# Attention scores and their maximum pass in two float32r pieces, two heads in the halves of the array

## Chip, cores and metric

One core of a Trainium2 chip. The time is the device time of one execution in microseconds (us), the median of several.

## What is computed

`x` is (2, 2048, 256) in float32. Its layer norm goes through causal attention with 16 heads of 16 channels, and through a gated feed-forward block; both are added to `x`.

```python
qkv = einsum('btd,ed->bte', xn, w_in); q, k, v = heads(split(qkv))   # 16 heads of 16
att = einsum('bhqd,bhkd->bhqk', q, k) / 4
att = where(causal, att, 0.0)          # a masked score is 0, not minus infinity
out = softmax(att) @ v                 # so masked keys carry weight exp(0 - max)
r = sigmoid(xr @ W_r.T); k = relu(xk @ W_k.T) ** 2; ffn = r * (k @ W_v.T)
return x + out @ w_out.T + ffn
```

`xr` and `xk` mix each token with the one before it. Since masked scores are 0, the softmax runs over all 2048 keys, and its maximum is at least 0 in every row but the last.

## The kernel before

It has two stages, each a block of five instruction streams that meet by semaphores.

**The token stage** (`stage_tokens`) takes 4096 tokens in 8 chunks of 512. For each it forms the layer norm, turns it, makes q, k and v, and runs the feed-forward block; its matmuls are float32. Scores need more precision than one bf16 gives, so each q and k value is kept as three bf16 parts: ScalarE casts the high part (L602), VectorE subtracts (L513), ScalarE casts the middle part (L607), VectorE subtracts again (L518). The parts go to DRAM (`parts_d`).

**The attention stage** (`stage_attention`) works through 8 groups of 4 heads (`group`; 2 batches by 4 groups; `G` counts them, `p` is the buffer half, the other half is loaded for the next group). A group has 4 query chunks `u` of 512. Chunk `u` needs `4 * (u + 1)` key tiles `kt` of 128, so there are 40 steps in a group. The tiles on the diagonal are narrower: 512, 384, 256 and 128 queries.

In a step TensorE computes for each of 4 heads a score tile (L1090): 128 keys by up to 512 queries, a contraction over 99 rows: 6 products of parts (`Q_PARTS`, `K_PARTS`) of 16 channels, and 3 rows which add the negated row maximum, in three bf16 parts, against rows of ones. The tiles go to three PSUM banks in turn (`SRING`). ScalarE takes the exponential of each into `probs` (L972), a ring of 16. On diagonal tiles POOL clears a triangle (L920). Two steps later (`LAG`) TensorE multiplies the values in (L1104), four heads side by side in column strips of 32, in float32; a further column of ones gives the denominator. Behind the third score of a step stands this value product.

**The maximum pass.** A row's maximum must be known before its scores are computed. So every score is computed a second time with queries in rows: a *piece* (L236) is 128 queries by up to 512 keys of one head, contraction over 96 rows, into one of three banks `ps_m` (`MRING`; two banks in the token stage). VectorE reduces each piece to a column of maxima: a plain reduction (L251), or on the diagonal a fused mask, add and maximum (L247) followed by a read of the accumulator. A group has 160 pieces: 96 off the diagonal, all 512 wide, and 64 on it, 16 each of 128, 256, 384 and 512. `pieces_of` puts the pieces of a slot evenly among its score tiles: one slot is each chunk, and the last chunk of a group carries the first 80 pieces of the next group. The first 80 of the first group are made in the last four chunks of the token stage (`pieces_beside_tokens`). A piece matmul waits for the reduction three pieces back (`piece_reduced`), and the next score is queued behind it in TensorE's order.

When the pieces of a chunk are reduced, six small VectorE steps (`max_step`, L260 to L280) form the maximum and its three parts; TensorE turns them (L1067, bf16), ScalarE copies them out (L953), SP writes them as rows into `q_op` (`place_shift`, L819). Before the first group this is done for chunks 0 and 1 with nothing beside it.

**Other work of a chunk.** The masked keys of a diagonal tile need weight exp(-max): POOL spreads that over 16 diagonal matrices (L887), TensorE multiplies them in (`masked_keys`, L1114, 32 instructions), behind the value product that ends the chunk. It needs sums of values over later keys (`sum_suffix`, L1081 and L1082, into bank `ps_x`). VectorE then divides by the denominator (L1007 to L1018), SP stores the rows (`attn_t`). In the last group the output tiles (L1136) follow.

**SP's queue in a group**: shift rows of chunk 2, then the loads of the next group's q, k and v once the first chunk's output is done, the normalised rows, shift rows of chunk 3, shift rows of chunks 0 and 1 of the next group.

## Time and profile before

| | us |
|---|---|
| median of 3 runs | 1230.48 (1223.11 to 1233.08) |
| profiled execution | 1224.13 |
| its span | 1222.3 |
| TensorE, VectorE, ScalarE, POOL busy | 1127.3, 949.4, 743.4, 347.7 |
| mean granted TensorE clock | 0.98 of 2.4 GHz |

Busy times are unions of the instructions' durations on an engine. A matmul's duration has its fill and drain in it, so that back-to-back matmuls overlap; what one costs is the distance from start to start. A wait is put down to what came last.

### The profile page before, as it was taken

The page shows a single profiled execution, that of the slowest core. Times are in us where ns is not written, and L with a number is a line of the kernel's source. Part 1 is how long each engine was busy: PE and PEld are TensorE (multiplying, and loading weights), DVE is VectorE, ACT ScalarE, POOL GpSimd, SP SyncE. Part 2 cuts the span into 40 slices and gives each one's busy share as a digit, 9 for nine tenths or more (in the row PEclk, how much of TensorE's full clock was granted, in tenths as well). Part 3 has the DMA queues.
Part 4 walks back from the last instruction along what each step waited for, and adds up shares of the span by engine and source line. Part 5 has one row for each costly group of instructions (what it writes and reads, how often), then busy time and mean ns, then how long its engine had stood idle before and what let it go on. Part 6 is the DMA issues. An engine that isn't in the chain of part 4 may idle for free.

```text
span 1222.3 us, 21443 instructions
## 1 busy us (share of the span) xinstructions
PE 1127.3 (92%) x7168; PEld 459.4 (38%) x7168; DVE 949.4 (78%) x2433; ACT 743.4 (61%) x1553; POOL 347.7 (28%) x716
## 2 busy tenths in 40 slices
PE   5889888789999999999999999999999999999998
PEld 3656544343333333333333333333233332333345
DVE  5757888778689858986888788778968986899623
ACT  3544433166766666667667766766677666666773
POOL 2212113132423232334132323332332233224121
PEclk9999999889999989999999999999999999999999
DMA  4577732309001900180028002700360045002033
GB/s 129 164 185 172 213 109 91 104 3 144 9 2 23 130 6 2 24 129 6 2 32 122 6 1 39 114 6 2 53 100 6 1 60 94 6 1 79 6 108 108
DMA packets 62353, 79.22 MB, mean 65 GB/s; under 512 B 7075, under 2 KB 52515, under 8 KB 61219
## 3 DMA queue, kind: packets, MB, share of 16 engines
q1 hardware_dynamic: 61091, 73.66, 30.1%
q0 software_dynamic: 1152, 4.19, 1.2%
q8 instruction: 57, 0.93, 0.3%
q14 instruction: 53, 0.43, 0.1%
HBM read 43.78 MB, written 29.36 MB: 60 GB/s over the span
## 4 chain that ended last, share of the span: by engine, by line
PE 49%; DVE 12%; DMA 9%; issue 4%; SPq 2%; POOL 2%; ACT 1%; DVEq 0%; POOLq 0%
PE ps_o L1104 15%; PE ps_s L1090 14%; PE ps_m L236 13%; DMA v_sb<-vpad_d 9%; DVE part_max L251 5%; DVE ps_m L247 3%; PE ps_m L1136 2%; PE ps_o L1114 2%; POOL after L228 2%; DVE row_max L264 1%; PE ps_x L1081 1%; DVE part_max L247 1%; PE ps_x L1082 1%; DVE turned L1007 1%; SPq L200 1%
## 5 line engine op out<-in xcount | busy, mean ns | idle before, releaser
L972 ACT ACTIVATE probs<-ps_s 128x512 f32<-128x512 f32 (+3 forms) x1280 | 610.2, 534 | 290.0 <-PE ps_s L1090 285.1
L251 DVE TENSOR_REDUCE part_max<-ps_m 128x1 f32<-128x512 f32 x730 | 473.8, 680 | 33.7 <-PE ps_m L236 32.2
L1090 PE MATMUL ps_s<-q_op,k_op 99*128 99x512 bf16 (+3 forms) x1280 | 431.1, 355 | 8.8 <-ACT probs L972 6.0
L236 PE MATMUL ps_m<-k_op,q_op 96*128 96x512 bf16 (+3 forms) x1200 | 402.5, 355 | 33.5 <-DVE part_max L251 23.4
L247 DVE CUSTOM_DVE_ANT_0 ps_m<-ps_m,mask 128x384 f32<-128x384 f32 x470 | 229.2, 496 | 122.1 <-PE ps_m L236 120.4
L1104 PE MATMUL ps_o<-probs,v_sb 128*32 128x512 f32 (+3 forms) x2560 | 303.0, 546 | 4.8 <-POOL probs L920 4.8
L920 POOL TENSOR_SCALAR_AFFINE_SELECT probs<-probs 128x128 f32<-128x128 f32 x512 | 143.2, 296 | 396.3 <-ACT probs L972 389.6
L1090 PEld LDWEIGHTS ps_s<-q_op,k_op 99*128 99x128 bf16 x1280 | 122.0, 98 | 325.2 <-ACT probs L972 219.3
L236 PEld LDWEIGHTS ps_m<-k_op,q_op 96*128 96x128 bf16 x1200 | 117.9, 98 | 199.4 <-DVE part_max L251 92.6
L887 POOL TENSOR_TENSOR diag_weight<-ident,masked_weight 128x2048 f32<-128x2048 f32 x32 | 115.5, 3610 | 121.2 <-ACT masked_weight L939 121.2
L1104 PEld LDWEIGHTS ps_o<-probs,v_sb 128*32 128x32 f32 x2560 | 50.8, 108 | 94.0 <-issue 36.7
L228 POOL TENSOR_TENSOR after<-after,v_sb 128x64 f32<-128x64 f32 x120 | 40.0, 333 | 134.2 <-DMA v_sb<-vpad_d 125.4
L247 DVE DVE_READ_ACCUMULATOR2_ANT part_max<- 128x1 f32 x512 | 71.6, 140 | 0.0
L670 PE MATMUL ps_qk<-xn_t,w_in_sb 128*128 128x512 f32 x128 | 60.6, 609 | 1.7 <-ACT xn_t L597 1.4
L441 POOL TENSOR_TENSOR k_act<-k_act 128x1024 f32<-128x1024 f32 x8 | 15.4, 1919 | 126.5 <-ACT k_act L635 126.5
L602 ACT ACTIVATE parts<-ps_qk 128x512 bf16<-128x512 f32 x32 | 19.0, 594 | 46.7 <-PE ps_qk L670 46.7
L236 PE MATMUL ps_pieces<-k_op,q_op 96*128 96x512 bf16 (+2 forms) x80 | 25.6, 355 | 18.4 <-DVE part_max L251 9.2
L446 POOL TENSOR_TENSOR ffn<-ffn,x_in 128x512 f32<-128x512 f32 x16 | 21.5, 1342 | 57.8 <-DVE ffn L525 57.8
L607 ACT CAST parts<-rest 128x512 bf16<-128x512 f32 x32 | 19.7, 616 | 28.9 <-DVE rest L513 28.9
L1114 PE MATMUL ps_o<-diag_weight,v_after 128*32 128x128 f32 x1024 | 37.2, 291 | 0.0
L670 PEld LDWEIGHTS ps_qk<-xn_t,w_in_sb 128*128 128x128 f32 x128 | 24.4, 196 | 26.8 <-issue 22.5
L1136 PE MATMUL ps_m<-w_out_sb,attn_t 128*128 128x256 f32 x128 | 31.6, 381 | 0.5 <-DVE v_sb L1025 0.5
(84 smaller groups left out, 819.7 us busy)
## 6 DMA issues: line engine op xcount, KB each, us to landing
parts_d<-parts SPq DMA_DIRECT2D x48, 256.0 KB, 3.2
q_op<-parts_d SPq DMA_DIRECT2D x42, 256.0 KB, 13.1
k_op<-parts_d SPq DMA_DIRECT2D x42, 256.0 KB, 15.2
vpad_d<-v_pad SPq DMA_DIRECT2D x32, 256.0 KB, 3.5
v_sb<-vpad_d SPq DMA_DIRECT2D x8, 1024.0 KB, 26.8
x_in<-x SPq DMA_DIRECT2D x8, 512.0 KB, 5.4
ffn_d<-ffn SPq DMA_DIRECT2D x8, 512.0 KB, 3.2
attn_t<-normed SPq DMA_DIRECT2D x128, 32.0 KB, 2.0
```

What stands on the lines that cost most here:

```text
L228: pool.tensor_tensor(self.after[:, j], self.after[:, j + 1], values[:, j + 1, :, 0:HD], ALU.add).then_inc(self.after_ready, 1)
L236: last = pe.matmul(ps_m[:, f % ring, 0:width], self.q_op[0:ROWS, p, h, q0:q0 + P], self.k_op[0:ROWS, p, h, pc * CH:pc * CH + width], start ...
L247: dve.tensor_tensor_reduce(ps_m[:, f % ring, 0:width], ps_m[:, f % ring, 0:width], self.mask16[:, CH - width:CH], 1.0, LOWEST, ALU.add, AL ...
L251: dve.tensor_reduce(self.part_max[:, u % 2, h * SUB + s, pc:pc + 1], ps_m[:, f % ring, 0:width], AX_X, ALU.max).then_inc(self.piece_reduce ...
L670: last = pe.matmul(ps_qk[:, j % 2], w_in_sb[:, cc, j * P:(j + 1) * P], xn_t[:, cc, 1:CH + 1], start=(cc == 0), stop=(cc == CC - 1))
L887: pool.tensor_tensor(diag_weight[:, u % 2], ident[:].unsqueeze(1).broadcast_to([P, GH * SUB, P]), masked_weight[:, u].unsqueeze(2).broadca ...
L920: pool.affine_select(out=blk, in_=blk, compare_op=ALU.is_ge, fill=0.0, base=0, pattern=[[1, P]], channel_multiplier=-1).then_inc(probs_mas ...
L972: act.activation(probs[:, slot % PRING, 0:width], ps_s[:, slot % SRING, 0:width], ACT.Exp).then_inc(probs_ready, 1)
L1090: pe.matmul(ps_s[:, slot % SRING, 0:CH - q0], k_op[0:KROWS, p, h, kt * P:(kt + 1) * P], q_op[0:KROWS, p, h, u * CH + q0:(u + 1) * CH], sta ...
L1104: last = pe.matmul(ps_o[h * HW:(h + 1) * HW, q0:CH], v_sb[:, p, kt, h * HW:(h + 1) * HW], probs[:, ((KT0[u] + kt) * GH + h) % PRING, 0:CH ...
L1114: last = pe.matmul(ps_o[h * HW:(h + 1) * HW, s * P:(s + 1) * P], v_after[:, p, u * SUB + s, h * HW:(h + 1) * HW], diag_weight[:, u % 2, h ...
L1136: last = pe.matmul(ps_m[:, k % MRING, 0:C], attn_t[:, b * CC + cc, c * CH + t * P:c * CH + (t + 1) * P], w_out_sb[:, cc], start=(cc == 0), ...
```

## The change

It does the following.

- q and k are kept as two parts, the high one rounded to float32r, the low one the difference. Three products of parts remain (0·0, 1·0, 0·1), 48 rows, and two shift rows: 50. The token stage loses L607 and L518.
- `q_op` and `k_op` are float32r. Heads 0 and 1 lie in rows 0 to 63, heads 2 and 3 in rows 64 to 127; a step takes the heads in the order 0, 2, 1, 3. The loads of a group stay 12 DMAs of 256 KB.
- A piece is now a pair: two matmuls (rows 64 up, then rows 0 up) into two neighbouring banks (`ps_m` has six), reduced by one VectorE instruction. A group has 80 pairs. The causal mask of diagonal pairs is added by TensorE: four small bf16 matmuls of 64 rows, 128 and 64 columns.
- `spread_pieces` spreads the pairs over all 80 half steps by width, 44 of them ahead of their group. A pair stands behind the first, or behind the third, score of a step. The first 44 are made from chunk 1 to chunk 7 of the token stage, in a ring of one pair.
- Masked keys, output tiles, suffix sums and shift transposes stand between the second and third score of a step. The latter two use the score banks; `ps_x` is gone. The value product stands behind the fourth score.
- The maximum takes three steps in place of six. The first two shifts are turned and placed during the token stage.
- SP loads the next q and k at the start of a group, ahead of the shift rows of chunk 2; v later, as before. POOL's spreading is 8 instructions in place of one. The Fori loops of the token stage are written out.

```diff
-Q_PARTS = (0, 1, 2, 0, 1, 0)
-K_PARTS = (0, 0, 0, 1, 1, 2)
+Q_PARTS = (0, 1, 0)
+K_PARTS = (0, 0, 1)
+HEAD_AT = (0, 2, 1, 3)
+def spread_pieces():
+    halves = [(u, kt, half) for u in range(NCH) for kt in range(key_tiles(u)) for half in range(HALVES)]
+    halves = halves[AHEAD_FROM * HALVES:] + halves[:AHEAD_FROM * HALVES]
+    room = [CH + 2 * (CH - first_query(u, kt)) for u, kt, _ in halves]
+    load = [P // 2 + piece(f)[4] for f in range(PIECES)]
...
-        self.q_op = sb("q_op", [P, 2, GH, T], BF16)
-        self.k_op = sb("k_op", [P, 2, GH, T], BF16)
+        self.q_op = sb("q_op", [P, 2, GH // 2, T], F32R)
+        self.k_op = sb("k_op", [P, 2, GH // 2, T], F32R)
...
     def score_piece(self, pe, ps_m, ring, f, p, base):
-        last = pe.matmul(ps_m[:, f % ring, 0:width], self.q_op[0:ROWS, p, h, q0:q0 + P],
-                         self.k_op[0:ROWS, p, h, pc * CH:pc * CH + width], start=True, stop=True)
+        for e in (1, 0):
+            rows = slice(e * HALF, e * HALF + ROWS)
+            last = pe.matmul(ps_m[:, f % ring * 2 + e, 0:width], self.q_op[rows, p, j, q0:q0 + P],
+                             self.k_op[rows, p, j, pc * CH:pc * CH + width], start=True, stop=(pc < u))
+        if pc == u:
+            for k in range(2):
+                for e in (1, 0):
+                    half = slice(e * HALF, (e + 1) * HALF)
+                    last = pe.matmul(ps_m[:, f % ring * 2 + e, s * P + k * HALF:width], self.pick16[half, k],
+                                     self.mask16[half, k, k * HALF:P], start=False, stop=(k == 1))
         last.then_inc(self.piece_ready, 1)
...
-            dve.tensor_tensor_reduce(ps_m[:, f % ring, 0:width], ps_m[:, f % ring, 0:width],
-                                     self.mask16[:, CH - width:CH], 1.0, LOWEST, ALU.add, ALU.max,
-                                     self.part_max[:, u % 2, h * SUB + s, pc:pc + 1]).then_inc(self.piece_reduced, 1)
+        dve.tensor_reduce(both, ps_m[:, bank:bank + 2, 0:width], AX_X, ALU.max).then_inc(self.piece_reduced, 1)
...
+                if not last:
+                    if not first:
+                        sp.wait_ge(scores_ready, (i * 2 + p) * SLOTS)
+                    ops.load_scores(sp, i + p, 1 - p)
...
-                pe.matmul(ps_s[:, slot % SRING, 0:CH - q0], k_op[0:KROWS, p, h, kt * P:(kt + 1) * P],
-                          q_op[0:KROWS, p, h, u * CH + q0:(u + 1) * CH], start=True, stop=True).then_inc(scores_ready, 1)
+                rows = rows_of(h, KROWS)
+                wait_for_bank("scores", slot, i, p, first, last)
+                pe.matmul(ps_s[:, bank_of("scores", slot, first, last), 0:CH - q0], k_op[rows, p, h % 2, kt * P:(kt + 1) * P],
+                          q_op[rows, p, h % 2, u * CH + q0:(u + 1) * CH], start=True, stop=True).then_inc(scores_ready, 1)
...
+                        for at in range(GH):
+                            score_tile(u, kt, at, i, p, first, last)
+                            some, ahead = pieces_at(u, kt, at // 2)
+                            if at % 2 == 0 and not (ahead and last):
+                                for f in some:
+                                    ops.score_piece(pe, ps_m, MRING, f, 1 - p if ahead else p, (G + ahead) * PIECES)
+                            if at == GH // 2 - 1:
+                                between_scores(i, p, u, kt, first, last)
```

## Rows read from the trace of the kernel before

**Rows 1.** The page's first part: busy time, share, instructions.
```profile
PE 1127.3 (92%) x7168; PEld 459.4 (38%) x7168; DVE 949.4 (78%) x2433; ACT 743.4 (61%) x1553; POOL 347.7 (28%) x716
```
**Rows 2.** Windows between maxima of chunk 3: length, busy by engine, clock, DMA, GB/s.
```profile
502.03:622.02 119.99, 114.45 (x812) 39.37 (x811) 101.27 (x270) 82.15 (x178) 38.60 (x84) 1.00 0.28 42
622.02:742.38 120.36, 114.38 (x804) 39.97 (x800) 99.86 (x265) 81.06 (x176) 37.01 (x84) 0.99 0.28 41
...
sum 723.51, PE 687.38 PEld 237.92 DVE 599.17 ACT 486.05 POOL 222.09; mean PE 114.56 PEld 39.65 DVE 99.86 ACT 81.01 POOL 37.02
```
**Rows 3.** Between the stages: timeline (start, us, instruction, idle before), then a window.
```profile
242.72 0.57 ACT L953 COPY shift_t<-ps_x 12x512 bf16<-12x512 bf16 x1 [13.19 <-PE ps_x L1067]
...
246.62 0.59 PE L1090 MATMUL ps_s<-q_op,k_op 99*128 99x512 bf16 x1 [2.59 <-DMA q_op<-shift_t]
...
240.00:250.00 10.00, 5.53 (x19) 2.28 (x19) 3.61 (x8) 4.85 (x9) 3.76 (x2) 0.50 0.01 2
```
**Rows 4.** Timeline of the end: the last run of output tiles.
```profile
1210.34 7.63 PEld L1136 LDWEIGHTS ps_m<-w_out_sb,attn_t 128*128 128x128 f32 x36 [0.94 <-DVE v_sb L1025]
1210.34 8.04 PE L1136 MATMUL ps_m<-w_out_sb,attn_t 128*128 128x256 f32 x36 [0.53 <-DVE v_sb L1025]
```
**Rows 5.** Timeline of a full step in the attention stage.
```profile
541.19 1.06 PE L1104 MATMUL ps_o<-probs,v_sb 128*32 128x512 f32 x8
...
542.18 0.39 PE L1090 MATMUL ps_s<-q_op,k_op 99*128 99x512 bf16 x1
...
542.41 0.38 PE L236 MATMUL ps_m<-k_op,q_op 96*128 96x512 bf16 x1
...
542.61 2.07 ACT L972 ACTIVATE probs<-ps_s 128x512 f32<-128x512 f32 x4 [0.67 <-PE ps_s L1090]
542.63 0.38 PE L1090 MATMUL ps_s<-q_op,k_op 99*128 99x512 bf16 x1
...
543.98 1.07 PE L1104 MATMUL ps_o<-probs,v_sb 128*32 128x512 f32 x8
```
**Rows 6.** Timeline: other matmuls and loads of TensorE, in tokens and groups.
```profile
152.16 1.88 PE L670 MATMUL ps_qk<-xn_t,w_in_sb 128*128 128x512 f32 x4
...
198.42 1.01 PEld L659 LDWEIGHTS ps_xt<-ident,xn 128*128 128x128 f32 x8
...
1131.79 1.06 PE L1114 MATMUL ps_o<-diag_weight,v_after 128*32 128x128 f32 x32
```
**Rows 7.** Groups by form, VectorE, 502.03 to 622.02: count, busy, mean ns, idle before.
```profile
L247 DVE CUSTOM_DVE_ANT_0 ps_m<-ps_m,mask 128x512 f32<-128x512 f32 x17 | 11.8, 696 | 1.1 <-PE ps_m L236 0.8
...
L247 DVE CUSTOM_DVE_ANT_0 ps_m<-ps_m,mask 128x128 f32<-128x128 f32 x16 | 4.7, 294 | 8.9 <-PE ps_m L236 8.9
```
**Rows 8.** Timeline of VectorE, pieces back to back.
```profile
593.46 1.28 DVE L251 TENSOR_REDUCE part_max<-ps_m 128x1 f32<-128x512 f32 x2
594.66 0.56 DVE L247 CUSTOM_DVE_ANT_0 ps_m<-ps_m,mask 128x384 f32<-128x384 f32 x1
595.13 0.14 DVE L247 DVE_READ_ACCUMULATOR2_ANT part_max<- 128x1 f32 x1
595.13 0.69 DVE L251 TENSOR_REDUCE part_max<-ps_m 128x1 f32<-128x512 f32 x1
```
**Rows 9.** The page's DMA issues: count, KB each, median us to landing.
```profile
k_op<-parts_d SPq DMA_DIRECT2D x42, 256.0 KB, 15.2
```
**Rows 10.** Timeline of ScalarE: the copies that open chunks 0, 1, 6, 7.
```profile
13.40 1.01 ACT L597 COPY xn_t<-ps_xt 128x1024 f32<-128x1024 f32 x1
...
37.30 1.01 ACT L597 COPY xn_t<-ps_xt 128x1024 f32<-128x1024 f32 x1
...
167.98 1.01 ACT L597 COPY xn_t<-ps_xt 128x1024 f32<-128x1024 f32 x1
...
199.94 1.01 ACT L597 COPY xn_t<-ps_xt 128x1024 f32<-128x1024 f32 x1
```
**Rows 11.** Waits: who waited for whom, us in total, times, longest.
```profile
PE ps_m L236 <- DVE part_max L251: 23.4, 44, 1.6
```

More of the change, by code:

```diff
@@ L104, in first_query, with pieces_at, score_uses, bank_of @@
     return P * max(0, kt - SUB * u)
+def spread_pieces():
[3 more added lines that the diff above has]
+    load = [P // 2 + piece(f)[4] for f in range(PIECES)]
+    behind = [sum(load[:f]) + load[f] // 2 for f in range(PIECES)]
+    until = [sum(room[:k + 1]) for k in range(len(halves))]
+    at = [next(k for k in range(len(halves)) if behind[f] * until[-1] < until[k] * sum(load)) for f in range(PIECES)]
+    return {where: [f for f in range(PIECES) if at[f] == k] for k, where in enumerate(halves)}
+SPREAD = spread_pieces()
+HEAD_START = sum(len(SPREAD[u, kt, half]) for u, kt, half in SPREAD if KT0[u] + kt >= AHEAD_FROM)
+def pieces_at(u, kt, half):
+    return SPREAD[u, kt, half], KT0[u] + kt >= AHEAD_FROM
+def score_uses(first, last):
+    uses = []
+    for u in range(NCH):
+        for kt in range(key_tiles(u)):
+            uses += [("scores", (KT0[u] + kt) * GH + at) for at in range(GH // 2)]
+            if first and (u, kt) in FIRST_SV_AT:
+                uses.append(("own suffix", FIRST_SV_AT[u, kt]))
+            if (u, kt) in SV_AT and not last:
+                uses.append(("suffix", SV_AT[u, kt]))
+            if (u, kt) in SHIFT_AT and not (u == NCH - 1 and last):
+                uses.append(("shift", SHIFT_AT[u, kt]))
+            uses += [("scores", (KT0[u] + kt) * GH + at) for at in range(GH // 2, GH)]
+    return uses
+def bank_of(what, which, first, last):
+    return (score_uses(first, last).index((what, which)) + 2 * first) % SRING
+def rows_of(h, rows):
+    return slice(h // 2 * HALF, h // 2 * HALF + rows)
+def pieces_beside_tokens(n, step):
+    def until(at):
+        return HEAD_START * min(max(0, at - PIECES_FROM), PIECES_UNTIL - PIECES_FROM) // (PIECES_UNTIL - PIECES_FROM)
+    return range(until(n * TOKEN_STEPS + step), until(n * TOKEN_STEPS + step + 1))
 def build(nc, x, w_in_t, w_r_t, w_k_t, w_v_t, w_out_t, mu_rk, out):
-    parts_d = nc.dram_tensor("parts_d", [3, 2 * B, C, T], BF16, kind="Internal").ap()
+    parts_d = nc.dram_tensor("parts_d", [2, 2 * B, C, T], F32, kind="Internal").ap()
     vpad_d = nc.dram_tensor("vpad_d", [B * NG, P, NT, GH * HW], F32, kind="Internal").ap()
@@ L580, in _ @@
             dve.wait_ge(mu_ready, 1)
-            with dve.Fori(0, B - 1) as b:
-                batch(b, False)
-            batch(B - 1, True)
+            for b in range(B):
+                batch(b, b == B - 1)
         @block.scalar
```

538 lines of the change are left out of this document (268 added, 270 removed).

## The prediction

> **What bounds the kernel now.** I read the busy shares of the page first. TensorE is busy for 1127 us of the 1222 us span, VectorE for 949 us [rows 1]. Both are near full as averages, so they don't yet say which one sets the pace. For that I cut the attention stage at the end of each group's piece work (the moment the row maximum of the fourth chunk is computed), which comes every 118 to 124 us, and read the windows between [rows 2]. In a group of 120.6 us (mean of six) TensorE is busy 114.6, VectorE 99.9 and ScalarE 81.0. Eight groups at 120.5 us make 964 us; the first score starts at 246.6 us [rows 3]; so 1222.3 - 246.6 - 964 = 11.7 us is the tail of output tiles, of which one run of 36 matmuls alone takes 8 us [rows 4].
>
> The timeline of one step (four heads by 128 keys by 512 queries) shows why TensorE is the bound [rows 5]. Scores start at 542.18 and 542.63 with a piece at 542.41 between them: 0.22 us from start to start, for 512 bf16 columns. The four value products (eight instructions, float32, four column strips side by side) start at 541.19 and the next score starts at 542.18: 0.99 us. Four scores, four pieces and the value products are 8 x 0.217 + 0.99 = 2.73 us, and the steps in this stretch come 2.8 us apart. The exponentials of four heads run back to back in 2.07 us, after which ScalarE had waited 0.67 us for a score. So a step ends when TensorE ends, and ScalarE's and VectorE's gaps are its shadow.
>
> **TensorE, what goes and what comes.** A group has 160 score and 160 piece matmuls, 69,632 columns each (112 of the scores are 512 wide, 16 each 384, 256 and 128; of the pieces 96 are 512 wide and 16 each of the four widths). At 0.217 us for 512 columns that is 29.5 us each, 59.0 together. The change contracts 48 or 50 rows in place of 96 or 99, and puts two heads into the two row halves, in strictly alternating order (score 0, piece 1, piece 0, score 2 and so on). Two things are not in this trace: a float32r matmul, and two row halves at once.
> - Side by side: the value products show tiles of the array working together. Their eight instructions take 0.99 us; a float32 instruction of 512 columns over the whole array takes 1.88 / 4, about 0.43 us from start to start [rows 6], so eight in turn would be 3.4 us. I take it that row halves do the same, since that is another cut of the same array.
> - Columns: bounds are 0.217 us per 512 (bf16) and 0.86 us (float32, two instructions of 0.43). A float32r matmul that needs one pass would stand with the first, and it is a single product of rounded numbers, which is why I take the bf16 end.
> - Weights: a bf16 load and its matmul fit into 0.217 us. For float32 the nearest row is the token transposes, eight loads and matmuls of 128 in 1.01 us: 0.124 us from start to start [rows 6]. If loads of both halves pass one after the other, a pair of matmuls takes 0.248 us, not 0.217.
>
> So scores and pieces of a group take 29.5 us (all hidden) to 320 x 0.124 = 39.7 us (loads bind everywhere). I take the middle, 34.7: it removes 24.3 us. The Trainium skill, TensorE: Matmul & The Clock Gate, section "Weight-path perf modes", speaks against the change here: the fast weight load is not given to FP32 operands, and LDWEIGHTS takes about its column count over 1.2. By it a pair would need 2 x 107 = 214 ns for its loads, just under the stream; the trace's 124 ns of load and matmul together agrees, and the sum by it would be 34 us in place of 34.7.
>
> Added: 32 of the 80 pairs of a group end on the diagonal and get four mask matmuls each, 128 in all, 128 or 64 columns wide. The nearest row is the masked keys product, 32 instructions in 1.06 us, 0.033 us each [rows 6]: 4.2 us; at the transposes' 0.124 us it would be 16. I take 0.05 us, 6.4 us, since they are short, bf16 and in two halves. The shift transposes turn from bf16 to float32: 16 at up to 0.124 us, 2 us a group if the bf16 ones had been free; I take 0.5. Masked keys, suffix sums and output tiles are moved between a step's second and third score and cost what they did. TensorE's own work falls by 24.3 - 6.9 = 17.4 us, from 114.6 to 97.
>
> **VectorE.** In the trace two full reductions take 1.28 us, 0.68 + 0.60, so 0.60 is what one occupies and a 384 wide diagonal piece occupies 0.47 (594.66 to 595.13), its accumulator read lying under the next instruction [rows 7, 8]. From the widths, 696 to 294 ns over 384 columns [rows 7], a column costs 1.05 ns. Before: 96 x 0.60 + 16 x (0.21 + 0.35 + 0.47 + 0.61) = 84 us, and 16 us for normalising and the maximum steps make the 99.9. After: one reduction over two banks replaces two; 1024 elements occupy 0.60 + 512 x 1.05 ns = 1.14. A group has 48 of them (54.7 us) and 8 each of 256, 512, 768 and 1024 (0.33 + 0.60 + 0.87 + 1.14 = 2.94, 23.5 us): 78.2 us. Three maximum steps of about 0.2 us go from each of four chunks, 2.4 us. The sum is 99.9 - 5.8 - 2.4 = 91.7 us. Below nothing is excluded, as the columns read are the same.
>
> **ScalarE** keeps its 160 exponentials: 81 us. The ring of three score banks now also carries suffix and shift products, eight uses in 168. Per step, score 3 waits for the exponential of score 0; then come 0.22 + 1.0 for score and value products, 0.4 until the next score is readable, 0.5 for its exponential: about 2.2 us, below what TensorE needs.
>
> **The period.** The three engines will stand at 97, 92 and 81 us where they stood at 114.6, 99.9 and 81.0 with a period of 120.6, 6 us above the largest. Since the first two are now within 5 us of each other, and each piece pair on TensorE waits for the reduction three pairs back with a score queued behind it, I add 7: 104 us. Both ends: 95 if loads are hidden (92) and waits cost 3; 113 if loads bind everywhere and masks cost 10 us (106 plus 7).
>
> **Queues.** The loads of the next q and k now stand ahead of the shift rows of chunk 2 in SP's queue: twelve DMAs of 256 KB, as many bytes as before, issued at the group's start. The shift rows are asked for about step 6 and needed at step 12, about 31 us into the group. I cost this at nothing, since the median k load landed 15.2 us after its issue [rows 9], half of the 31; if it is late, the first score of chunk 2 waits, all engines with it. POOL's weights are spread in eight parts, behind the same wait: nothing.
>
> **Token stage.** Chunks without pieces come 23.9 us apart (13.40 to 37.30), those with 24 pieces 32.0 apart (167.98 to 199.94) [rows 10]: 0.34 us for a piece. After, 44 pairs are spread over chunks 1 to 7. At 0.34 to 0.68 us for a pair, 37 pairs before the last chunk are 13 to 25 us, less a little for a cast and a subtraction gone from each of four tiles a chunk. The last chunk starts at 13.4 + 7 x 23.9 + 16 = 197 and takes 24 + 4 + 3 = 31 us: 228. Then the shift is already turned and placed, so that the stretch in which ScalarE waits 13.2 us for it and the granted clock is 0.50 (the 1.2 GHz level, after TensorE had been little busy) is gone [rows 3]: the first score at 228, not 246.6. Bounds 220 and 240. In the groups TensorE would show 97 of 104 us busy, 93%, where it shows 95% now with 0.99 to 1.00 granted [rows 2], so I take 2.4 GHz there.
>
> **Sum.** 228 + 8 x 104 + 11.7 = 1072 us of span. The profiled execution took 1224.1 us against a span of 1222.3, and the median of the runs is 1230.5, 6 us above: I add 8 and say 1080 us.
>
> **Rivals.**
> - *The pair takes as long as two in turn* (halves not side by side, or 0.21 us for a float32r load, as in the run of 36 loads in 7.63 us, which bounds it from above [rows 4]): scores and pieces stay at 59 us, TensorE is at 121, its period about 122: 228 + 976 + 12 + 8 = 1224, no change. For it: no row shows row halves together. Against: the value products.
> - *Float32r streams like float32* (the other side). Side by side, 0.43 us a matmul instead of 0.108: 118 us for scores and pieces, TensorE 185 us a group, 1700 us; with two cycles in place of four 59 us, again 1224. It decides against the change from 0.22 us a matmul on. Against it stands the single product; no row of this trace does.
> - *Waits take the gain*: VectorE at 92 us and the mask matmuls' latency hold the piece pairs, scores queue behind them, or the shift rows of chunk 2 come late by several us: a period of 111 to 117, 1136 to 1184 us. For it: TensorE's piece matmuls already wait 23.4 us for full reductions [rows 11].
> - *TensorE leaves the bound*: loads hidden, masks at 0.033: 92 us, VectorE at 92; a period of 95 to 98 and 1008 to 1032.
>
> **Chances.** The forecast (period 99 to 110, 1040 to 1128) 0.53; waits take the gain 0.19; leaves the bound 0.11; pair in turn 0.11; slow float32r 0.06. What a measurement can tell from no change is about 1%, 12 us. The three first cases are all faster, 0.83; of the pair in turn 0.08 is within 1% and the rest split, so faster 0.84, same 0.08, slower 0.08. The range is 1010 to 1190: it leaves out the two last cases and some of the best one, under 2 in 10.
>
> **What would show it.** Right: score and piece in opposite halves start together or within 0.13 us; reductions of 2 x 512 last 1.2 us; TensorE busy 95 to 100 us of a group of 104; the first score near 228 with the clock at 1.0. Wrong: start to start of 0.2 us or more in a pair, two instructions for each float32r matmul, mask matmuls of over 0.1 us each, a score waiting for the shift rows' DMA, a granted clock below 0.95 in the groups, or VectorE gaps that name the pieces.

## The result and the profile after

The changed kernel takes 1178.4 us (median; 1176.6 to 1179.9) against 1231.8 for the kernel before, measured together: a ratio of 0.957, interval 0.952 to 0.963. The forecast was 1080. The direction was right; of the 150 us foreseen 53 came. Two of the experiments below (e1, e5) have no ratio, since their executions differ by more than 3% with the granted clock.

The page of the kernel after: busy times as in [rows 1], then four of the costliest groups (busy us, mean ns of one | idle before, releaser). L1154 is the score, L302 the piece, L309 its mask, L1168 the value product, L319 the reduction, L1021 the exponential.

```profile
PE 1105.7 (94%) x8192; PEld 552.7 (47%) x8192; DVE 849.9 (72%) x1153; ACT 722.8 (61%) x1519; POOL 384.8 (33%) x945
...
L1021 ACT ACTIVATE probs<-ps_s 128x512 f32<-128x512 f32 (+3 forms) x1280 | 607.0, 535 | 270.7 <-PE ps_s L1154 266.5
L319 DVE TENSOR_REDUCE part_max<-ps_m 128x2 f32<-128x1024 f32 (+2 forms) x596 | 618.6, 1062 | 190.3 <-PE ps_m L302 128.2
...
L302 PE MATMUL ps_m<-k_op,q_op 48*128 48x512 f32 (+3 forms) x1192 | 358.7, 428 | 29.7 <-DVE part_max L319 28.9
...
L302 PEld LDWEIGHTS ps_m<-k_op,q_op 48*128 48x128 f32 x1192 | 171.9, 191 | 60.4 <-DVE part_max L319 57.4
```

The windows from one maximum of chunk 3 to the next, cut as in [rows 2] (columns as there):

```profile
522.63:642.03 119.40, 113.47 (x931) 53.29 (x929) 91.95 (x108) 81.28 (x176) 41.57 (x111) 0.93 0.29 42
642.03:756.22 114.19, 108.58 (x932) 51.35 (x930) 91.13 (x108) 80.58 (x176) 41.57 (x111) 0.99 0.30 43
...
sum 697.72, PE 663.63 PEld 312.49 DVE 548.29 ACT 484.97 POOL 247.78; mean PE 110.60 PEld 52.08 DVE 91.38 ACT 80.83 POOL 41.30
```

The mean of six is 697.72 / 6 = 116.3 us a group, where [rows 2] gave 120.6 and the forecast was 104. VectorE's 91.4 us and ScalarE's 80.8 stand where they were forecast. TensorE's 110.6 does not (97 forecast). 8 x 12.3 = 98 us, as much as lies between 1080 and 1178. That the sum closes so well is luck: the first score came 4 us late, the end took 4 us more, and the 8 us added for the median were not needed. The period is what has to be explained.

The first score, in the timeline after (it was at 246.62 in [rows 3]):

```profile
231.81 0.76 PE L1154 MATMUL ps_s<-q_op,k_op 50*128 50x512 f32 x1 [5.51 <-PEq L352]
```

TensorE had been idle for 5.5 us between the stages. The granted clock is 0.50 from 228.4 us on for 17 us. Before, it was 0.50 for 14 us from 236.7 and again for 3 us from 264. So that stretch is not gone, as the prediction had it; it has moved behind the first score.

### The profile page after: what moved, and what is told of

The parts are those of the page before. It is cut to its first block, busy times and chain, and to the rows that moved or that the text cites. A ratio compares the mean times of both kernels' runs of the same rounds, so it can differ in the third digit from the quotient of the medians.

```text
span 1178.0 us, 21912 instructions
## 1 busy us (share of the span) xinstructions
PE 1105.7 (94%) x8192; PEld 552.7 (47%) x8192; DVE 849.9 (72%) x1153; ACT 722.8 (61%) x1519; POOL 384.8 (33%) x945
## 4 chain that ended last, share of the span: by engine, by line
PE 65%; DVE 10%; ACT 3%; issue 3%; ACTq 0%; DVEq 0%
PE ps_s L1154 22%; PE ps_o L1168 22%; PE ps_m L302 9%; DVE part_max L319 7%; PE ps_o L1179 3%; ACT probs L1021 3%; PE ps_m L1199 3%; PE ps_s L1143 2%; PE ps_m L309 2%; PE ps_s L1144 1%; PE ps_s L1133 1%; DVE turned L1065 0%; DVE normed L1070 0%; DVE turned L1059 0%; DVE shift L334 0%
## 5 line engine op out<-in xcount | busy, mean ns | idle before, releaser
L1021 ACT ACTIVATE probs<-ps_s 128x512 f32<-128x512 f32 (+3 forms) x1280 | 607.0, 535 | 270.7 <-PE ps_s L1154 266.5
L319 DVE TENSOR_REDUCE part_max<-ps_m 128x2 f32<-128x1024 f32 (+2 forms) x596 | 618.6, 1062 | 190.3 <-PE ps_m L302 128.2
L1154 PE MATMUL ps_s<-q_op,k_op 50*128 50x512 f32 (+3 forms) x1280 | 462.8, 437 | 17.5 <-ACT probs L1021 7.7
L302 PE MATMUL ps_m<-k_op,q_op 48*128 48x512 f32 (+3 forms) x1192 | 358.7, 428 | 29.7 <-DVE part_max L319 28.9
L1154 PEld LDWEIGHTS ps_s<-q_op,k_op 50*128 50x128 f32 x1280 | 213.3, 190 | 332.3 <-ACT probs L1021 225.8
L1168 PE MATMUL ps_o<-probs,v_sb 128*32 128x512 f32 (+3 forms) x2560 | 306.7, 552 | 0.0
L302 PEld LDWEIGHTS ps_m<-k_op,q_op 48*128 48x128 f32 x1192 | 171.9, 191 | 60.4 <-DVE part_max L319 57.4
L934 POOL TENSOR_TENSOR diag_weight<-ident,masked_weight 128x256 f32<-128x256 f32 x256 | 150.3, 623 | 49.0 <-ACT masked_weight L987 49.0
L309 PE MATMUL ps_m<-mask,pick 64*128 64x128 bf16 (+1 forms) x936 | 98.7, 211 | 0.0
L1168 PEld LDWEIGHTS ps_o<-probs,v_sb 128*32 128x32 f32 x2560 | 51.1, 109 | 76.6 <-issue 43.0
L319 DVE TENSOR_REDUCE part_max<-ps_pieces 128x2 f32<-128x1024 f32 (+3 forms) x44 | 44.4, 1009 | 42.1 <-PE ps_pieces L302 23.5
L309 PEld LDWEIGHTS ps_m<-mask,pick 64*128 64x128 bf16 x936 | 46.4, 97 | 10.1
L1179 PEld LDWEIGHTS ps_o<-diag_weight,v_after 128*32 128x32 f32 x1024 | 29.9, 122 | 12.8 <-issue 7.8
```

The lines of the kernel that those rows point to most:

```text
L302: last = pe.matmul(ps_m[:, f % ring * 2 + e, 0:width], self.q_op[rows, p, j, q0:q0 + P], self.k_op[rows, p, j, pc * CH:pc * CH + width], s ...
L309: last = pe.matmul(ps_m[:, f % ring * 2 + e, s * P + k * HALF:width], self.pick16[half, k], self.mask16[half, k, k * HALF:P], start=False, ...
L319: dve.tensor_reduce(both, ps_m[:, bank:bank + 2, 0:width], AX_X, ALU.max).then_inc(self.piece_reduced, 1)
L934: pool.tensor_tensor(diag_weight[:, u % 2, some], ident[:].unsqueeze(1).broadcast_to([P, GH * SUB // DIAGS, P]), masked_weight[:, u, some] ...
L1021: act.activation(probs[:, slot % PRING, 0:width], ps_s[:, bank_of("scores", slot, first, last), 0:width], ACT.Exp).then_inc(probs_ready, 1)
L1154: pe.matmul(ps_s[:, bank_of("scores", slot, first, last), 0:CH - q0], k_op[rows, p, h % 2, kt * P:(kt + 1) * P], q_op[rows, p, h % 2, u * ...
```

## Where a group's time went

A full step in the timeline after, to be held against [rows 5]:

```profile
565.97 0.40 PE L1154 MATMUL ps_s<-q_op,k_op 50*128 50x512 f32 x1
...
566.30 1.07 PE L1168 MATMUL ps_o<-probs,v_sb 128*32 128x512 f32 x8
567.29 0.18 PEld L1154 LDWEIGHTS ps_s<-q_op,k_op 50*128 50x128 f32 x1 [0.84 <-issue]
567.29 0.50 PE L1154 MATMUL ps_s<-q_op,k_op 50*128 50x512 f32 x1
567.30 0.29 PEld L302 LDWEIGHTS ps_m<-k_op,q_op 48*128 48x128 f32 x2
567.30 0.49 PE L302 MATMUL ps_m<-k_op,q_op 48*128 48x512 f32 x1
...
567.63 0.39 PE L1154 MATMUL ps_s<-q_op,k_op 50*128 50x512 f32 x1
567.64 0.40 PE L302 MATMUL ps_m<-k_op,q_op 48*128 48x512 f32 x1
```

A score and a piece in opposite halves start 0.01 us apart (567.29 and 567.30, then 567.63 and 567.64): the halves do work at once. But the first pair behind the value product occupies 0.34 us, not 0.23, and it lasts 0.50 where later ones last 0.40.

The table counts TensorE's time from each matmul's start to the next one's, worked out from the starts in the trace and put down to the kind of the earlier one. It has waits in it, which busy time lacks. "Before" is the group 548 to 668 and "after" the one from 642 to 756, both at a clock of 0.99; the last columns are two experiments told of below, in groups at a clock of 1.00 (394 to 499 and 376 to 475).

| us of a group | before | after | e7 | e10 |
|---|---|---|---|---|
| scores and pieces | 76.0 | 58.7 | 50.6 | 44.1 |
| masks of pieces | | 8.9 | 8.7 | 7.4 |
| value products | 34.4 | 34.8 | 35.4 | 36.7 |
| masked keys | 4.9 | 4.9 | 4.0 | 4.1 |
| shift rows, suffix sums | 4.7 | 6.8 | 6.4 | 6.4 |

Scores and pieces fell by 17.3 us where 24.3 were taken off. The masks cost 8.9 for 6.4, shift rows and suffix sums 2.1 more for 0.5. With 0.4 more for the value products that makes -5.8 in this group. The mean of the groups is 2.1 us longer than this one: the clock, below.

## The experiments

Period means here the mean distance of the eight maxima of chunk 3 in the profiled execution: 120.5 before, 116.0 after (seven distances; the 116.3 above is the mean of the six windows shown in part). The clock is that of the whole profiled execution. The profiled execution of b1 was its slowest, 1224.9 us.

| | median us | ratio to before | period | mean clock |
|---|---|---|---|---|
| changed kernel | 1178.4 | 0.957 (0.952 to 0.963) | 116.0 | 0.968 |
| the same again (e12) | 1183.6 | 0.967 (0.962 to 0.971) | 116.8 | 0.961 |
| e1 no masks | 1190.1 | | 116.8 | 0.947 |
| e2 one row half | 2073.4 | 1.688 (1.683 to 1.693) | | 0.575 |
| e3 half exponentials | 1165.8 | 0.950 (0.946 to 0.954) | 113.8 | 0.966 |
| e4 half reductions | 1128.3 | 0.919 (0.917 to 0.922) | 108.9 | 0.989 |
| e5 values behind third score | 1251.3 | | 124.3 | 0.929 |
| e6 pieces behind second | 1197.6 | 0.978 (0.971 to 0.986) | 117.5 | 0.983 |
| e7 = e3 + e4 | 1105.5 | 0.899 (0.894 to 0.905) | 106.7 | 0.978 |
| e8 spread in one | 1247.9 | 1.017 (1.011 to 1.024) | 125.9 | 0.930 |
| b1 before, spread in eight | 1214.0 | 0.990 (0.984 to 0.995) | 120.3 | 0.978 |
| e9 spread by a select | 1171.7 | 0.958 (0.952 to 0.963) | 115.0 | 0.976 |
| e10 = e7 with bf16 | 1043.8 | 0.852 (0.847 to 0.857) | 99.3 | 0.978 |
| e11 select in one | 1192.4 | 0.974 (0.969 to 0.979) | 118.0 | 0.970 |
| e13 = e7 without masks | 1093.6 | 0.893 (0.891 to 0.896) | 104.7 | 0.975 |
| e14 normalising spaced | 1179.9 | 0.964 (0.961 to 0.966) | 115.8 | 0.977 |
| e16 = e14 + select | 1178.7 | 0.963 (0.960 to 0.966) | 116.3 | 0.975 |

### Do the halves work at once (e2)?

```diff
-    return slice(h // 2 * HALF, h // 2 * HALF + rows)
+    return slice(0, rows)                      # likewise in score_piece
```

> The changed kernel with all scores and pieces in rows 0 to 63 (heads 2 and 3 then read the rows of heads 0 and 1; that part is changed), so nothing can start side by side. Theory A (side by side is what the change gains on TensorE; 194 of 320 matmuls of a group start with a partner, each pair saves 0.2 us): the period rises by about 97 x 0.2 = 19 us or more, 1330 us. Theory B (waits hide it): under 60 us more, below 1240. If fp32r loads can't run ahead within one half, more than 1400.

It took 2073 us, far above what theories A and B gave. Only the last of the three expectations (more than 1400) has room for it, but the reason is another one. The page and a window of it:

```profile
PE 2045.2 (99%) x8192; PEld 1085.1 (52%) x8192; DVE 867.0 (42%) x1153; ACT 777.1 (37%) x1519; POOL 386.9 (19%) x945
...
PEclk9999855555555555555555555555555555555569
```
```profile
900.00:1100.00 200.00, 200.00 (x826) 105.39 (x825) 81.31 (x94) 76.81 (x156) 39.04 (x107) 0.50 0.16 24
```

TensorE has no idle time in this window and yet the granted clock is 0.50, the 1.2 GHz level; it is so from 238 to 2003 us but for 3 us. So the time of e2 does not price the two halves against two in turn at one clock. That they run together is shown by the rows above (0.01 us apart).

The starts in e2 allow an estimate. In its one half, full matmuls that follow each other come 0.43 us apart at this clock, twice the 0.22 of [rows 5], and scores and pieces fill 138 us of the group 811 to 1044. At twice the clock that would be 69 us, where e7, below, has 50.6 in two halves. So side by side is worth some 18 us a group, and a column of float32r streams as fast as one of bf16.

Why the clock stayed down was not tried. What differed from the changed kernel is that rows 64 to 127 of the array took no part in scores, pieces and masks, and that TensorE never paused.

### What do the masks cost (e1, e13)?

```diff
-        if pc == u:
+        if False:
```

> The changed kernel without the four small mask matmuls of each diagonal pair, so its maxima are taken over later keys too (that part is left out). In the changed kernel 9.0 us of a group's TensorE starts lie behind a mask matmul. Theory A (the masks are plain work of TensorE, which sets the pace): the period falls from 116.3 by 7 to 9 us, 60 to 70 us in all, 1110 to 1120 us. Theory B (the pace is set by waits between engines, above all the fourth score's wait for the exponential of the first, the masks fill time that would be waited anyway): under 25 us, 1155 or more.

The fastest execution took 1168.9 us at a clock of 0.972, the one with the profile 1188.0 at 0.947. Only the first can be set beside 1178.4 at 0.968: that one execution puts the masks at some 10 us of the 71 (8 x 8.9) that their starts fill. It is what theory B gave (under 25 us).

> Halved exponentials and reductions (1105 us) and no mask matmuls (masks left out). 9.0 us of a group's TensorE starts lie behind mask matmuls. If the masks cost only that when nothing else holds TensorE: 9 us a group less, 1030 to 1040. If the return from bf16 masks to float32r opens a load as well (132 of 224 full-width matmuls of a group last 0.48 or more in place of 0.39): 10 to 13 us a group less, 1000 to 1030 us, and the long ones fall to about 80. If they fill gaps even here: above 1060.

With the reductions and exponentials halved, removing them gives 12 us of 1105.5, 2.0 us of the period, far above 1060 as in the last of the three cases. In a group at a clock of 1.00 (390 to 493) scores and pieces fill 55.7 us where e7 has 50.6. So most of what the masks' starts fill is not won back without them.

### Who else holds the group (e3, e4, e7)?

```diff
-        dve.tensor_reduce(both, ps_m[:, bank:bank + 2, 0:width], AX_X, ALU.max)      # e4, e7
+        dve.tensor_reduce(both, ps_m[:, bank:bank + 2, 0:width // 2], AX_X, ALU.max)
...
-                            act.activation(probs[:, slot % PRING, 0:width], ps_s[..., 0:width], ACT.Exp)   # e3, e7
+                            act.activation(probs[:, slot % PRING, 0:width // 2], ps_s[..., 0:width // 2], ACT.Exp)
```

> The changed kernel with each exponential over half its columns (the other half of the weights stays at a zero set once at the start, about 9 us extra). ScalarE then needs some 40 us less a group. Theory B (the fourth score waits for the first exponential in the ring of three, starts alone and pays its load in the open): the period falls by 8 to 15 us, 1060 to 1120 us. Theory A (TensorE's own work sets the pace): under 3 us a group, 1155 to 1185 with the extra 9.

> The changed kernel with each reduction over half the columns (the maxima of the other half are left out). VectorE then has about 45 of 116 us busy instead of 91. Theory C (the ring of two piece pairs holds TensorE, which waits 28.9 us in all for reductions): the period falls by 4 to 8 us, 1115 to 1145 us. Theory B alone: under 2 us a group, 1165 to 1180.

> Halved exponentials and halved reductions at once (what both leave out is the other half of the columns; about 9 us extra for setting the weights to zero once). Neither ScalarE nor VectorE can hold TensorE then, so the period shows TensorE's own work. The prediction put that at 97 us, here 1028 us with the 9. If TensorE's own work is larger than the prediction had it (loads in the open after each change of tiling, masks at 9 us): period 103 to 107, 1075 to 1110 us. Halving only the reductions gave 1128 us.

Halving the reductions brings 50 us, within what theory C gave. Halving the exponentials brings 1178 - 1166 = 13, as theory A had it. e3 and e7 need a memset behind the first score, of 6.9 us. From the first score to the first maximum of chunk 3 they take 3 and 5 us longer than the changed kernel and e4, which lack it, so some 3 to 9 us more would be theirs. Both together bring 73, as e7's expectation had it. The reductions of e4 in the page:

```profile
L319 DVE TENSOR_REDUCE part_max<-ps_m 128x2 f32<-128x512 f32 (+2 forms) x596 | 355.7, 612 | 402.3 <-PE ps_m L302 267.7
...
L302 PE MATMUL ps_m<-k_op,q_op 48*128 48x512 f32 (+3 forms) x1192 | 349.5, 410 | 7.9 <-DVE part_max L319 4.7
```

TensorE's wait for reductions goes from 28.9 to 4.7 us, half of the gain. Its loads wait less too (57.4 to 16.0 us for L302, in part beside running matmuls), and the clock is 0.989 in place of 0.968: it falls once in the seven groups, not in each. What these two bring was not taken apart. VectorE is only 72% busy after, so it is not full. It is late in places.

But even e7 has a period of 106.7, where TensorE's own work was forecast at 97. Of the 12.3 us that a group is over the forecast, 9.7 are still there when VectorE and ScalarE have half their work. The 97 was a busy time, though. TensorE is busy 103.5 us of a group in e7 (mean of seven groups), so 6.5 of the 9.7 are work beyond the forecast and 3.2 are gaps that the halving did not close.

### Is it float32r (e10)?

```diff
-            last = pe.matmul(..., self.q_op[rows, p, j, q0:q0 + P], self.k_op[rows, p, j, ...], ...)
+            last = pe.matmul(..., self.q_op[rows, p, j, q0:q0 + P].bitcast(BF16)[:, 1::2],
+                             self.k_op[rows, p, j, ...].bitcast(BF16)[:, 1::2], ...)   # scores alike
```

> Halved exponentials and reductions as in the run that gave 1105 us, and scores and pieces read the high 16 bits of each float32r value as bf16, every second element (the numbers lose their low bits; that part is changed), same rows, same halves, same order. Tells apart what float32r costs when no other engine holds TensorE. If float32r pays for its load in the open at each change of tiling (first pair after a value product 0.33 us until the next where the stream alone is 0.22): 0.1 us x 40 to 60 a group, 4 to 6 us a group, 1057 to 1075. If the stream of float32r were slower than bf16 too: below 1050. If the drain at a change of tiling costs the 0.1 whatever the type: 1098 to 1110.

It is 62 us faster than e7; the period is 99.3 in place of 106.7. That is more than the first case gave, and by the time alone it is the second (below 1050, a slower stream). The starts decide against a slower stream. First e7's timeline behind a value product, then e10's:

```profile
601.27 0.50 PE L1159 MATMUL ps_s<-q_op,k_op 50*128 50x512 f32 x1
601.27 0.29 PEld L302 LDWEIGHTS ps_m<-k_op,q_op 48*128 48x128 f32 x2
601.28 0.49 PE L302 MATMUL ps_m<-k_op,q_op 48*128 48x512 f32 x1
...
601.61 0.40 PE L1159 MATMUL ps_s<-q_op,k_op 50*128 50x512 f32 x1
```
```profile
605.67 0.11 PEld L302 LDWEIGHTS ps_m<-k_op,q_op 48*128 48x128 bf16 x2
605.67 0.40 PE L1159 MATMUL ps_s<-q_op,k_op 50*128 50x512 bf16 x1
...
605.91 0.39 PE L1159 MATMUL ps_s<-q_op,k_op 50*128 50x512 bf16 x1
```

In bf16 two loads end within 0.11 us and the next score starts after 0.24. In float32r one load lasts 0.19, two take 0.29, and the next score starts after 0.34. So a load of 128 float32r columns occupies 0.10 us of the load path, a bf16 one almost nothing, and a score's start waits for its load where nothing covers it. In a run of pairs two loads (0.20) fit under the 0.23 to 0.24 from pair to pair, which both types have.

Both kernels run the same instructions in the same order, so that their groups (394 to 499, 376 to 475) can be laid side by side from one value product to the next, 39 times. A step without other products is mostly 0.18 to 0.20 us shorter in bf16: 0.10 behind the value product, and 0.10 on the way to the next, where a last score waits for its own load. A step with shift, suffix or masked-key products in it is mostly 0.29 to 0.33 shorter, since the first pair behind these starts with an open load too. 36 of the 39 steps add up to 7.9 us; in two others e10 waits 0.8 and 1.0 us longer. Open loads at the changes from one kind of matmul to another are so enough for all of the 7.4 us. The 62 us are float32r's price with the work of the other two engines halved; in the full kernel it was not measured.

### Are scores without a partner the loss (e5, e6)?

In the group of the table 83 of 160 scores and 111 of 160 pieces start within 0.02 us of a partner, a score or piece in the other half.

```diff
-                            if at == GH - 1:
+                            if at == GH - 2:      # e5: value product behind the third score
...
-        for e in (1, 0):
+        for e in (0, 1):                          # e6, and pairs behind scores 2 and 4
-                            if at % 2 == 0 and not (ahead and last):
+                            if at % 2 == 1 and not (ahead and last):
```

> The changed kernel with the value product behind a step's third score again, as in the kernel before, in place of behind the fourth. In the changed kernel 77 of 160 scores of a group start without a partner; the fourth, which has to wait for the first exponential, is most of them. Theory B (broken pairs: the wait in the ring of three score banks makes the fourth score start alone and pay 0.33 us instead of 0.11): now the wait is covered by the value product and the fourth starts beside the next first score, 3 to 6 us a group less, 1130 to 1155 us. Theory C (the wait for VectorE in the ring of two piece pairs sets the pace): within 1%, 1166 to 1190.

> The changed kernel with the piece pairs behind the second and fourth score of a step (halves in the order 0, 1) in place of the first and third: scores then start as a pair and pieces as a pair, and a piece that waits for VectorE holds up one score less. Theory B: 1 to 4 us a group less, 1145 to 1170 us. Theory C: VectorE gets the same work as late or later, no gain, 1170 to 1195 us.

Both failed as remedies, and neither theory had their times. e5 starts 105 scores with a partner and is slower at any clock (1228 us at its fastest; its group at a clock of 1.00 takes 116.4 us, where the changed kernel's take 114 at 0.99). e6 has 106 scores and 132 pieces with a partner and takes 1198. The exponentials in the page of e5:

```profile
L1021 ACT ACTIVATE probs<-ps_s 128x512 f32<-128x512 f32 (+3 forms) x1280 | 603.3, 536 | 345.8 <-PE ps_s L1154 339.9
```

ScalarE waits 340 us for scores there against 266.5 after. TensorE's scores wait 27 us for a bank to be read by an exponential in e5 and 34 in e6, where they wait 8 after; its pieces wait less for reductions, 19 and 15 us where it was 28.9. I read from this that the order decides when a bank of scores comes free, and that it outweighs the filling of pairs. The lack of a partner is not what costs the time that e4 gives back: e4 has 88 scores and 104 pieces with one.

### POOL's spreading and VectorE (e8, b1, e9, e11)

```diff
-DIAGS = 8
+DIAGS = 1                  # e8, e11
...
-                    pool.tensor_tensor(diag_weight[...], ident[...], masked_weight[...], ALU.mult)
+                    pool.affine_select(out=diag_weight[...], in_=masked_weight[...], compare_op=ALU.is_equal,
+                                       fill=0.0, pattern=[[0, ...], [-1, P]], channel_multiplier=1)   # e9, e11
```

> The changed kernel with POOL's spreading of the masked weights as one instruction again, in place of eight. In the changed kernel VectorE's small steps between 592 and 596 us take 0.66 and 0.88 us beside the eight (4.79 us) where they take about 0.21 and 0.44 alone, TensorE waits 2.25 us behind them for a reduction, and the clock falls to 0.50 right after. If the eight parts cost VectorE more than one of 3.6 us did: 5 to 15 us less, 1163 to 1173. If the collision is the same either way: within 4 us of 1178. If a long instruction holds VectorE longer: 1185 or more.

> The kernel before with one part of the change alone: POOL's spreading in eight parts. In the changed kernel undoing that part cost 70 us. If the collision with VectorE works the same way here (a VectorE step of two inputs waits for the end of a POOL instruction of 3.6 us; the row maximum step took 1.54 us once a group): 10 to 30 us less, 1200 to 1220. If it matters only where the ring of piece pairs is short: within 1% of 1228.

> The changed kernel with the diagonal matrices made by a select over a broadcast of the weights (one input) in place of a multiplication with the identity (two inputs), in eight parts as before. Theory D (POOL and VectorE hold each other up when both run an instruction with two inputs from SBUF, and the late normalising steps hold the pieces, then the scores, then the clock): VectorE's division goes from a mean of 0.61 to about 0.44 us, the clock to 0.98 or more, 15 to 35 us less, 1143 to 1163. If it is only that POOL is busy: within 1% of 1178.

> The same select as one instruction for all 16 matrices. Theory D: a select doesn't hold VectorE however long it is, so as fast as in eight parts, 1140 to 1165. If any long POOL instruction holds VectorE: near the 1248 us of the single multiplication.

The edit that the prediction passed over with one word is worth 70 us in the changed kernel, more than its whole gain, and 1% (12 us) in the kernel before. e8's timeline:

```profile
618.96 3.61 POOL L934 TENSOR_TENSOR diag_weight<-ident,masked_weight 128x2048 f32<-128x2048 f32 x1
618.97 3.65 DVE L334 SCALAR_TENSOR_TENSOR shift<-row_max,shift 128x16 f32<-128x16 f32 x1
...
622.53 0.41 DVE L1065 TENSOR_TENSOR turned<-turned,inv_denom 128x256 f32<-128x256 f32 x1
...
624.86 0.79 PE L302 MATMUL ps_m<-k_op,q_op 48*128 48x512 f32 x2 [4.77 <-DVE part_max L319]
```

A VectorE instruction on 16 columns (median of its 32: 182 ns) starts 0.01 us behind POOL's, lasts 3.65 us and ends about with it; TensorE then waits 4.77 us for a reduction. The division of the normalising, in e8, after and before, shows the same over 32 instructions each:

```profile
L1065 DVE TENSOR_TENSOR turned<-turned,inv_denom 128x256 f32<-128x256 f32 x32 | 57.9, 1808 | 0.0
```
```profile
L1065 DVE TENSOR_TENSOR turned<-turned,inv_denom 128x256 f32<-128x256 f32 x32 | 19.4, 607 | 0.0
```
```profile
L1013 DVE TENSOR_TENSOR turned<-turned,inv_denom 128x256 f32<-128x256 f32 x32 | 14.2, 443 | 0.1
```

In e8 14 divisions start beside the spreading and take 44 us in all beyond their median of 0.42; the longest lasts 3.85. In the kernel before the same 3.6 us of POOL met another step of VectorE, the row maximum, 8 times: 12 us in all, at most 2.2 for 0.17. The reductions, which read PSUM, last 1063 ns in e8 as after. The Trainium skill, SBUF — State Buffer, section "SBUF: two separate sides", says that a VectorE instruction with two SBUF inputs and a GpSimd one share a port pair under an exclusive lock, held for the whole instruction. Both held instructions have two SBUF inputs, and the traces agree.

A select reads one tensor and takes 415 ns for a part in place of 623, but e9 has the ratio of the changed kernel: no gain that can be told from noise, as was expected if POOL is merely busy, and divisions of 518 ns where theory D had 440. In one piece (2005 ns) the select costs 21 us against e9, between the two expectations. 7 of 32 divisions then last over 1 us, up to 2.22, and so do 7 of 32 of the shift steps, up to 2.03. So a POOL instruction with one input holds VectorE as well, for as long as it lasts; theory D was wrong to except it. What hurts is one long POOL instruction.

### Is it the burst at a chunk's end (e14, e16)?

In the timeline after, TensorE's longest wait of a group, 74 us into it:

```profile
593.22 4.79 POOL L934 TENSOR_TENSOR diag_weight<-ident,masked_weight 128x256 f32<-128x256 f32 x8
593.23 0.66 DVE L334 SCALAR_TENSOR_TENSOR shift<-row_max,shift 128x16 f32<-128x16 f32 x1
...
593.81 0.88 DVE L1065 TENSOR_TENSOR turned<-turned,inv_denom 128x256 f32<-128x256 f32 x1
...
594.72 0.71 DVE L1070 STREAM_TRANSPOSE normed<-turned 128x512 f32<-128x512 f32 x1
595.36 1.52 DVE L319 TENSOR_REDUCE part_max<-ps_m 128x2 f32<-128x1024 f32 x2
...
596.60 0.50 PE L302 MATMUL ps_m<-k_op,q_op 48*128 48x512 f32 x2 [2.25 <-DVE part_max L319]
```

A maximum step, POOL's spreading and the normalising meet on VectorE; both pairs of banks of the ring stay full; scores are queued behind the piece, and ScalarE waits 2.20 us as well. Behind it the clock falls. Windows of 4 us (the fraction of 2.4 GHz stands ahead of the DMA share):

```profile
592.00:596.00 4.00, 2.27 (x21) 1.24 (x20) 3.97 (x6) 2.32 (x7) 3.78 (x9) 1.00 0.99 111
596.00:600.00 4.00, 3.40 (x24) 1.39 (x28) 2.43 (x4) 1.29 (x3) 2.01 (x4) 0.63 1.05 119
600.00:604.00 4.00, 4.00 (x49) 2.52 (x39) 2.13 (x2) 2.06 (x4) 0.00 (x0) 0.50 1.00 115
604.00:608.00 4.00, 4.00 (x20) 1.20 (x19) 2.65 (x4) 2.86 (x6) 0.00 (x0) 0.50 1.03 117
...
616.00:620.00 4.00, 4.00 (x32) 1.53 (x29) 3.58 (x3) 2.94 (x8) 2.21 (x9) 1.00 0.05 10
```

It falls at this place in each group, for 3 to 17 us. The group 522 to 642, with the long fall, takes 119.4 us at a mean clock of 0.93; the next takes 114.2 at 0.99.

```diff
-                        norm, between = divmod(hs - NORM_AT, HALVES)
+                        norm, between = divmod(hs - NORM_AT, 2 * HALVES if u else HALVES)   # e14, e16
```

> The changed kernel with VectorE's four normalising steps every fourth instead of every second score, in chunks 1 to 3. If VectorE's bursts are what holds the ring of two piece pairs: 5 to 20 us less than the changed kernel on the same chip. If VectorE's sum over a chunk is what counts: within 4 us of it.

> Both of the small relieves of VectorE: the normalising steps spaced and the diagonal matrices by a select (alone 1172 us, ratio 0.958). If both hold: 1145 to 1160. If VectorE's sum counts: 1168 to 1176.

> The changed kernel once more, unchanged, so that the others of this call have it on the same chip: 1172 to 1185 us.

Beside the changed kernel run again (1183.6), spacing gives 4 us and both edits 5, and the intervals of the three ratios overlap. By e14's expectation that speaks for VectorE's sum (e16's time is above both of its ranges). But the spacing did not take the wait away. TensorE's matmuls wait 34.8 us for reductions in e14, up to 2.3 at a time, and 32.1 in e16, where they wait 28.9 in e12. So these runs show that the two edits bring next to nothing; whether e4's 50 us come from the sum of VectorE's work or from its clustering stays open.

## Why the prediction was off

**What held.** The halves work together; VectorE 91.4 (91.7 forecast), ScalarE 80.8 (81), a reduction over 1024 lasting 1.22 us (1.2). The last chunk of the token stage starts at 197.25 (197), the first score at 231.8 (228). Shift rows and the earlier loads kept nobody waiting in a group. First score, eight periods and the end leave 1178.0 - 231.8 - 8 x 116.3 = 15.8 us against 11.7, and from the profiled span to the median is 0.4 us, not 8. These three misses cancel.

**Step 1 that failed: "TensorE's own work falls by 17.4 us", to 97.** Terms of this sum were mis-sized. In e7 TensorE is busy 103.5 us of a group, 6.5 above. Masks are 2.3 of it (8.7 for 6.4) and shift rows and suffix sums 1.2 (1.7 more for 0.5). The loads of float32r cost 7.4 (e7 against e10), where "scores and pieces 34.7" had 34.7 - 29.5 = 5.2 for them: 2.2 more. These three make 5.7; it is an estimate, since they are taken from starts and the 6.5 from a busy time. The size of the load term was near, its mechanism was not. The prediction had it hidden or 0.124 us for each of 320 equal instructions, and took the middle. A group has no such even stream: it has 40 value products, and the load is in the open behind each and ahead of each. So of float32r's 62 us some 42 (8 x 5.2) were in the forecast. With bf16 operands TensorE is busy 93.9 us, where the forecast without its load term is 92. Step 1 is 8 x 6.5 = 52 of the 98 us. e13 shows that taking the masks out gives back only 2.0 us a group.

**Step 2 that failed: "I add 7" for waits.** The period stands 116.3 - 103.5 = 12.8 us above TensorE's own work, so that this term is short by 8 x 5.8 = 46 us. Of the 12.8, 116.3 - 106.7 = 9.6 go when the other two engines' work is halved. I had reasoned with a reduction "three pairs back". That was misread: the ring of the changed kernel is two pairs deep (`MRING = 2`, four banks, where the text ahead says six), beside three banks of scores, and one for values. A pair of banks gives TensorE at most one reduction (1.1 us) of slack, as I read it; no run varied the depth. The rival "waits take the gain" had the right time (1136 to 1184) and part of the cause: VectorE holds the pairs and scores queue behind, as it said, and halving its reductions gives back 50 us (e4). Of its other causes, the masks brought some 10 us at most (e1) and late shift rows were not there. It also took TensorE's own work as forecast, which it was not.

**Step 3: clock at 2.4 GHz.** In the groups it was not constant: one fall a group behind a wait of some 2 us. The groups with a fall of 3.4 us take 114 us, those with 17 take 119; over the mean period that is 2.1 us, part of the 12.8 above. And the stretch at 0.50 between the stages did not go with its cause: it lasted 17 us behind the first score.

**Step 4: the spreading, "nothing".** Its 3.6 us stood in the trace before, where it held the row maximum for up to 2.2, and what it would meet was not asked. Without the split the change would be slower than before (e8, 1.7%): the rival on the other side that the prediction should have named. Its condition is that POOL's long instruction falls onto VectorE's two-input ones. That VectorE has then two pairs of slack instead of three pieces was not tested apart.

One slip changes nothing: with 118 us for scores and pieces, TensorE's sum in the rival of a slow float32r is 97 - 34.7 + 118 = 180, not 185.

**Left open.** e13 halves the other engines' work, has no masks, and still has a period of 104.7. In its group at a clock of 1.00 value, shift, suffix and masked-key products fill 47 us of 103, and scores and pieces 55.7. 320 matmuls in perfect pairs would fill 35, an estimate with 0.23 us for a full pair and 0.20, two loads, for a narrower one. Nearly half of the 21 between them lies at one place: the 40 scores that stand ahead of a value product fill 13.9 us, 0.35 each, where half a pair is 0.11. The rest was not taken apart, nor were deeper rings tried, since all eight banks are used. No kernel tried was clearly faster than the changed one: e9's 1171.7 is the lowest full one, at the same ratio.

## What to carry to other kernels

Price an operand type by what its load costs at the breaks of the stream, not within it: count how often a step changes to another kind of matmul, and put one open load on the way into it and one on the way back. When one engine is sped up until another stands within 10% of it, ask first how many buffers lie between the two and take the wait from that depth, not from the gap in the sums. And look at every long instruction on POOL as a lock that an instruction of VectorE may run into: list what can start beside it.

## What the runs showed of the hardware that I had not expected

- A float32r load of 128 columns lasts 0.19 us where a bf16 one lasts 0.10, and two in a row take 0.29 against 0.11 (e7, e10). The Trainium skill, TensorE: Matmul & The Clock Gate, gives a load the time of its columns over 1.2 (section "LDWEIGHTS (loading the stationary operand)"), 0.107 us for 128. FP32 operands get no fast load (section "Weight-path perf modes"). The 0.10 from load to load agrees, if float32r counts as FP32 there.
- TensorE busy without a gap, with only rows 0 to 63 used in scores, pieces and masks, was granted 0.50, the 1.2 GHz level, from the start of the attention stage to near its end (e2, 238 to 2003 us; mean 0.575).
- POOL's multiplication of 3.61 us stretched a VectorE instruction on 16 columns to 3.65 us, where the median is 0.18 (e8), and did nothing to reductions out of PSUM (1063 ns against 1062). A select of 2.0 us with one input stretched the same instruction to 2.03 us (e11).
